# Layer 0 of a two-layer transformer: attention scores moved from one masked 104-row contraction to four 32-row tiles, with queries and keys laid out through DRAM

## What is computed

```python
xn = layernorm(x)                       # no gain, no bias
q = xn @ Wq.T; k = xn @ Wk.T; v = xn @ Wv.T
qh = q.reshape(b, s, 4, 8, 8)           # 4 query heads for each of 8 key heads, head size 8
kh = k.reshape(b, s, 8, 8); vh = v.reshape(b, s, 8, 8)
probs = softmax(einsum('bsqhd,bthd->bqhst', qh, kh) / sqrt(8))
a_dot = einsum('bqhst,bthd->bsqhd', probs, vh)
sigma = elu(q); a_mem = (sigma @ memory) / (sigma @ memory_norm)
x = x + a_dot * (1 - w) + a_mem * w + ffn(xn)   # ffn: 4-bit weights, gelu(gate) * up, hidden 2048
```

## Time and profile before

| | |
|---|---|
| median of 3 runs | 842.98 us (842.37 to 846.78) |
| profiled execution | 845.34 us, span 843.4 us |
| layer 0's units in the trace | unit 0 begins at 28.3 us, unit 63 at 589.2 us |
| TensorE busy | 741.0 us, 88% of the span |
| VectorE, ScalarE, GpSimd busy | 632.9, 468.3, 424.2 us |

### The profile page before, as it was taken

How to read it: one execution, slowest core, us unless ns; L and a number is a source line. 1 busy time by engine, 2 the same in 40 slices (tenths; PEclk the granted TensorE clock), 3 DMA queues, 4 the chain that set the end, 5 groups by cost and what they waited for, 6 DMA issues and landing times. The chain is left out here.

```text
span 843.4 us, 15160 instructions
## 1 busy us (share of the span) xinstructions
PE 741.0 (88%) x5602; PEld 637.2 (76%) x5602; DVE 632.9 (75%) x1099; ACT 468.3 (56%) x746; POOL 424.2 (50%) x369
## 2 busy tenths in 40 slices
PE   3368799999999999999999999999788898889773
PEld 2256678888888887888888888888666687777562
DVE  6989877787777676677768768665264898989865
ACT  4246645655655665564665565657675555565411
POOL 2344354354356566657535434436546373764821
PEclk9579999999999999999999999999979999999985
DMA  5111121111011010110100000021100000000000
GB/s 157 28 39 39 39 77 47 35 50 46 3 33 38 23 40 24 49 40 26 27 10 14 22 2 21 21 78 39 40 14 0 1 1 26 1 26 1 1 26 25
DMA packets 22108, 25.89 MB, mean 31 GB/s; under 512 B 4498, under 2 KB 17170, under 8 KB 22036
## 3 DMA queue, kind: packets, MB, share of 16 engines
q1 hardware_dynamic: 22036, 24.93, 10.4%
HBM read 14.83 MB, written 3.28 MB: 21 GB/s over the span
## 5 line engine op out<-in xcount | busy, mean ns | idle before, releaser
L652 DVE TENSOR_REDUCE neg_max<-s_pair 128x4 f32<-128x1024 f32 x127 | 154.9, 1220 | 75.5 <-PE s_pair L866 75.3
L474 ACT ACTIVATE probs<-t_pair 128x1024 f32<-128x1024 f32 x128 | 131.3, 1025 | 136.4 <-PE t_pair L891 136.2
L371 POOL TENSOR_TENSOR hid<-g,hid 128x512 f32<-128x512 f32 x64 | 82.1, 1283 | 177.8 <-DVE g L763 144.7
L365 POOL TENSOR_TENSOR hid_lo<-hid,hid_hi 128x512 fp32r<-128x512 f32 x64 | 85.5, 1336 | 82.8 <-ACT hid_hi L497 82.7
L866 PE MATMUL s_pair<-K,Q 96*128 96x256 f32 x508 | 85.0, 291 | 15.6 <-DVE neg_max L652 9.3
L866 PEld LDWEIGHTS s_pair<-K,Q 96*128 96x128 f32 x508 | 75.8, 195 | 24.2 <-issue 8.1
L891 PE MATMUL t_pair<-Q,K 104*128 104x512 f32 x256 | 86.2, 418 | 0.3 <-DMA Q<-max_parts 0.3
L933 PE MATMUL down<-hi,hid_hi 128*128 128x256 f32 x256 | 83.9, 328 | 0.8 <-POOL hid_lo L365 0.8
L906 PE MATMUL misc<-probs,V 128*32 128x256 f32 x1024 | 69.4, 389 | 3.3 <-DVE kc L608 2.6
L933 PE MATMUL down<-lo,hid_hi 128*128 128x256 f32 x256 | 71.5, 279 | 0.0
L933 PE MATMUL down<-hi,hid_lo 128*128 128x256 f32 x256 | 71.3, 278 | 0.0
(11 more groups left out here) (258 smaller groups left out, 1964.8 us busy)
## 6 DMA issues: line engine op xcount, KB each, us to landing
stage<-in_ternary SPq DMA_DIRECT2D x18, 256.0 KB, 2.8
Q<-q_hi SPq DMA_DIRECT2D x64, 64.0 KB, 2.0
stage<-in_scales SPq DMA_DIRECT2D x8, 384.0 KB, 3.4
X<-in_x SPq DMA_DIRECT2D x8, 256.0 KB, 4.2
Q<-q_lo SPq DMA_DIRECT2D x32, 64.0 KB, 2.0
Q<-max_parts SPq DMA_DIRECT2D x128, 4.0 KB
out<-X SPq DMA_DIRECT2D x8, 256.0 KB, 2.2
signs<-w_stage SPq DMA_DIRECT2D x9, 128.0 KB, 1.8
```

Of the source, the lines that this page charges most:

```text
L365: pool.tensor_tensor(hid_lo[:, m % 2, :, :].rearrange("p a n -> p (a n)"), hid[:, m % 2, :], hid_hi[:, m % 2, :, :].rearrange("p a n -> p ...
L371: pool.tensor_tensor(hid[:, m % 2, :], g[:, m % 2, :], hid[:, m % 2, :], ALU.mult).then_inc(S["hid_done"], 1)
L474: act.activation(probs[:, u % 2, th, :], t_pair[:], ACT.Exp, scale=SCALE).then_inc(S["probs_done"], 1)
L652: dve.tensor_reduce(neg_max[:, u % 2, 4 * jp:4 * jp + 4], score_banks(u, jp)[:].rearrange("p (s n) -> p s n", n=SEQ), AX_X, ALU.max, negat ...
```

## The change

The scores use row tiles. `Q` and `K` now hold, for each of the 8 key heads, four groups of 32 partitions, one for each query head: 24 rows (three parts x 8) and two for maxima. A score matmul contracts 24 rows of one group, a transposed one 26. So `scores` still has 4 matmuls of 256 columns for each jp, and `scores_turned` now goes by jp and has 4 of 256 columns in place of 2 of 512. To fill this layout, SyncE stores the query parts (6 DMAs) and the keys (1 DMA) of a batch to DRAM and loads each quad with 8 DMAs; GpSimd's masking is gone. Maxima are placed by 4 DMAs in place of 2, and no longer wait for the previous unit. In TensorE's order turn_max(u + 1) comes after the whole gate product, and scores(u + 2, 1) comes last, next to scores_turned(u + 1, 0). VectorE does normalised(u - 1) ahead of maximum(u + 2, 1). The exponential writes the same elements in another order. The weight columns are permuted on the host to match.

The diff, cut:

```diff
@@ schedule @@
-    for kind in ("stats", "norm", "turn", "q", "qlow", "kv", "qload0", "mask0", "qload1", "mask1"):
+    for kind in ("stats", "norm", "turn", "q", "qlow", "kv", "qstore", "kstore", "load0", "load1"):
         put(FIRST, kind, 0)
...
-        for n, kind in ((0, "stats"), (1, "norm"), (2 + late, "turn"), (3 + late, "q"), (4 + late, "qlow"), (4 + late, "qload0"), (4 + late, "kv"),
-                        (5, "mask0"), (5, "recip0"), (6, "recip1"), (8, "qload1"), (8, "mask1")):
+        for n, kind in ((0, "stats"), (1, "norm"), (2 + late, "turn"), (3 + late, "q"), (4 + late, "qlow"), (4 + late, "qstore"), (4 + late, "kv"), (4 + late, "kstore"),
+                        (5 + late, "load0"), (5, "recip0"), (6, "recip1"), (8, "load1")):
@@ layer0, buffers @@
-        Q = sb("Q", [P, 2, QPK, SEQ], F32R)
-        K = sb("K", [P, 2, QUAD, SEQ], F32R)
+        Q = sb("Q", [P, HEADS, SEQ], F32R)
+        K = sb("K", [P, HEADS, SEQ], F32R)
@@ SyncE @@
-            def place_queries(b, quad):
...
-                for r, part in ((0, q_hi), (2, q_hi), (1, q_lo)):
...
-                        sp.dma_start(dst.bitcast(F32), part[src, :, :].bitcast(F32)).then_inc(q_placed[quad], 16)
+            def store_queries(b):
+                sp.wait_ge(S["q_parts"], 3 * b + 1)
...
+                for part, x in ((0, q_hi), (2, q_hi), (1, q_lo)):
+                    if part == 1:
+                        sp.wait_ge(S["q_lo_done"], b + 1)
+                    for jj in range(2):
+                        dst = dram["q_parts"][b % 2, jj::2, DKV * part:DKV * part + DKV, :].rearrange("c e n -> e c n")
+                        sp.dma_start(dst.bitcast(F32), x[DKV * jj:DKV * jj + DKV, :, :].bitcast(F32)).then_inc(S["q_stored"], 16)
+            def store_keys(b):
+                sp.wait_ge(S["kc_lo_done"], b + 1)
...
+                sp.dma_start(dram["k_parts"][b % 2].bitcast(F32), kc[0:KROWS, :, :].bitcast(F32)).then_inc(S["k_stored"], 16)
+            def place_heads(b, quad):
+                if b > 0:
+                    sp.wait_ge(S["st_done"], 2 * (HEADS * (b - 1) + QUAD * quad + QUAD))
+                heads = slice(QUAD * quad, QUAD * quad + QUAD)
+                sp.wait_ge(S["q_stored"], 96 * (b + 1))
+                for r in range(QPK):
+                    src = dram["q_parts"][b % 2, r].rearrange("(e h) n -> e h n", h=HEADS)[:, heads, :]
+                    sp.dma_start(Q[32 * r:32 * r + HROWS, heads, :].bitcast(F32), src.bitcast(F32)).then_inc(qk_placed[quad], 16)
...
+                sp.wait_ge(S["k_stored"], 16 * (b + 1))
+                for r in range(QPK):
+                    src = dram["k_parts"][b % 2].rearrange("(e h) q n -> e q h n", h=QUAD)[:, quad]
+                    sp.dma_start(K[32 * r:32 * r + HROWS, heads, :].bitcast(F32), src.bitcast(F32)).then_inc(qk_placed[quad], 16)
             def place_max(u):
-                if u > 0:
-                    sp.wait_ge(S["st_done"], 2 * u)
...
-                for part in range(2):
-                    sp.dma_start(Q[row + part:row + part + 1, h // QUAD, :, :].rearrange("a q (s n) -> a (q s) n", n=P).bitcast(F32),
-                                 max_parts[:, part, :].bitcast(F32)).then_inc(S["placed"], 16)
+                if u >= HEADS:
+                    sp.wait_ge(S["st_done"], 2 * (u - HEADS) + 2)
+                for s in range(2):
+                    for part in range(2):
+                        sp.dma_start(Q[HROWS + part:P:32, h, P * s:P * s + P].bitcast(F32),
+                                     max_parts[QPK * s:QPK * s + QPK, part, :].bitcast(F32)).then_inc(S["placed"], 16)
@@ GpSimd @@
-                elif kind in ("mask0", "mask1"):
...
-                    pool.tensor_tensor(K[0:KROWS, quad, :, :], src, mask, ALU.mult).then_inc(k_masked[quad], 1)
@@ ScalarE @@
+            act.wait_ge(S["zeroed"], 5)
+            act.activation(K[:].rearrange("p h n -> p (h n)"), ones[:, 0:1].to_broadcast([P, HEADS * SEQ]), ACT.Copy).then_inc(S["rows_set"], 1)
@@ VectorE, the unit loop @@
+                if attends(u - 1):
+                    normalised(u - 1)
                 if attends(u + 2):
                     maximum(u + 2, 1)
                 if u == FIRST + 1:
                     weights_low(0)
-                if attends(u - 1):
-                    normalised(u - 1)
@@ TensorE, scores @@
                 if jp == 0 and hq == 0:
-                    pe.wait_ge(q_placed[quad], 96 * (b + 1))
-                    pe.wait_ge(k_masked[quad], b + 1)
+                    pe.wait_ge(qk_placed[quad], 128 * (b + 1))
...
-                for j in range(2):
-                    for s in range(2):
-                        mm = pe.matmul(score_banks(u, jp)[:, 512 * j + SEQ * s:512 * j + SEQ * s + SEQ], Q[0:KROWS, quad, 2 * jp + j, P * s:P * s + P],
-                                       K[0:KROWS, quad, hq, :], start=True, stop=True)
+                for s in range(2):
+                    for j in range(2):
+                        rows = slice(32 * (2 * jp + j), 32 * (2 * jp + j) + HROWS)
+                        mm = pe.matmul(score_banks(u, jp)[:, 512 * j + SEQ * s:512 * j + SEQ * s + SEQ], Q[rows, h, P * s:P * s + P], K[rows, h, :], start=True, stop=True)
@@ TensorE, scores_turned @@
-                for jp in range(2):
-                    mm = pe.matmul(t_pair[:, 512 * jp:512 * jp + 512].rearrange("p (j n) -> p j n", j=2), K[rows, quad, hq, P * th:P * th + P],
-                                   Q[rows, quad, 2 * jp:2 * jp + 2, :], start=True, stop=True)
+                for th in range(2):
+                    for j in range(2):
+                        rows = slice(32 * (2 * jp + j), 32 * (2 * jp + j) + HROWS + MROWS)
+                        mm = pe.matmul(t_pair[:, 512 * j + SEQ * th:512 * j + SEQ * th + SEQ], K[rows, h, P * th:P * th + P], Q[rows, h, :], start=True, stop=True)
@@ TensorE, the unit loop @@
-                    hidden_product(m, 0, gate, S["gate_done"], u + 1 if attends(u + 1) else None)
-                elif attends(u + 1):
+                    hidden_product(m, 0, gate, S["gate_done"])
+                if attends(u + 1):
                     turn_max(u + 1)
                 before = steps(u)
...
                 if 0 <= m - BEHIND < M:
                     down_product(m - BEHIND, 0)
-                if attends(u + 2):
-                    scores(u + 2, 1)
                 if attends(u - 1):
                     turn_out(u - 1)
                 if 0 <= m - BEHIND < M:
                     down_product(m - BEHIND, 1)
+                if attends(u + 2):
+                    scores(u + 2, 1)
```

More of the change, by code:

```diff
@@ L60 @@
 KROWS = 3 * QUAD * DH
-MROWS = 2 * QUAD
+HROWS, MROWS = 3 * DH, 2
 CW = WORDS // 2
@@ L178, in layer0 @@
         S = {n: ctx.enter_context(nc.semaphore(f"a_{n}")) for n in names}
-        q_placed, k_masked = ([S[f"{n}{i}"] for i in range(2)] for n in ("q_placed", "k_masked"))
+        qk_placed = [S[f"qk_placed{i}"] for i in range(2)]
         stage_sem = [S[f"stage{i}"] for i in range(2)]
@@ L267, in _ @@
                 for kind, n in at.get(u, []):
-                    if kind in ("qload0", "qload1"):
-                        place_queries(n, int(kind[-1]))
+                    if kind == "qstore":
+                        store_queries(n)
+                    elif kind == "kstore":
+                        store_keys(n)
+                    elif kind in ("load0", "load1"):
+                        place_heads(n, int(kind[-1]))
                 a = u + 3
@@ L399, in _ @@
                 for kind, n in at.get(u, []):
-                    if kind == "mask1" and u == FIRST:
+                    step(kind, n)
+                    if kind == "qlow" and u == FIRST:
                         weights_low(0)
-                    step(kind, n)
                     if kind == "recip0" and u == -1:
@@ L429, in step @@
                     if b > 0:
-                        for quad in range(2):
-                            act.wait_ge(k_masked[quad], b)
+                        act.wait_ge(S["k_stored"], 16 * b)
                         act.wait_ge(S["v_turned"], b)
@@ L446, in query_parts @@
                 if b > 0:
-                    for quad in range(2):
-                        act.wait_ge(q_placed[quad], 96 * b)
+                    act.wait_ge(S["q_stored"], 96 * b)
                     act.wait_ge(S["sigma_done"], 2 * b)
@@ L657, in split_max @@
                 if u > 0:
-                    dve.wait_ge(S["placed"], 32 * u)
+                    dve.wait_ge(S["placed"], 64 * u)
                 dve.tensor_copy(max_parts[:, 0, :], misc[0:8, 2 * P:3 * P]).then_inc(S["dve_link"], 1)
@@ L878, in turn_max, with scores_turned @@
                 pe.transpose(misc[0:8, 2 * P:3 * P], neg_max[:, u % 2, :], ident[:]).then_inc(S["max_turned"], 1)
[L880 removed]
+            def scores_turned(u, jp):
                 b, h = divmod(u, HEADS)
                 quad, hq = divmod(h, QUAD)
[L883 to L892 removed]
+                if jp == 0:
```

(30 more changed lines are left out.)

59 lines of the change are left out of this document (17 added, 42 removed).

## The result

871.39 us in the median of four runs (866.85 to 872.38) against 844.88 (842.37 to 847.71, four runs here, three in the table ahead). The ratio is 1.0305, 95% interval 1.0259 to 1.0352: slower by 3%. The profiled executions are 866.85 (span 865.1) and 845.34 (span 843.4), 21.7 apart in span. Forecast was +38, measured +26.5 between the medians.

The account below looks back on a forecast made before the run. Past the first units TensorE's own work was taken to bound the kernel. Terms -26 + 28 + 2 + 17 + 8 + 7 + 5 - 3 = +38 gave 881 us for the median, range 850 to 922.

Parts of the forecast that it names:

- late turn: Steps behind turn_max after the whole gate product start later: +0.71 us in 40 units past the first six, +28 us.
- row stretches: Two TensorE stretches of 8 score matmuls per unit, 0.73 us each, replace 1.90 us: -26 us over units 6 to 63.
- third wave: Each stretch of 8 score matmuls was counted as three waves of 0.118 us, 0.35, plus 0.38 around them.
- loads of batches 2 to 7: TensorE waits 2.9 us ahead of each such batch's first scores for queries and keys through DRAM: +17 us.
- Turn_out: Turn_out loses scores(u+2, 1) as its cover, and ScalarE's copy is late where VectorE is: +2 us in all.
- Unit 6: Batch 1's load0 stands behind place_max(7) in the very iteration that needs it: +8 us.
- separate term for the clock: Seven stops of 3 to 8 us bring three falls of the granted clock: +5 us (0 to 12).
- Start: First scores wait for stores and loads through DRAM until 26.2 us, VectorE's decoding behind them: +7 us, all counting.
- GpSimd: Without masks GpSimd has the sigmas earlier, so one or two waits ahead of mem go: -3 us.
- waits smaller, stretches at 0.6: Rival: loads issue at 0.43 us, no clock falls, stretches at 0.6: 851 us; smaller waits or cheaper stretches, chance 0.12.

Follow-up runs that it names:

- experiment 1: The kernel before, with only turn_max moved behind the whole gate product: 881.57 us, ratio 1.0447 to the kernel before.
- experiment 2: The changed kernel's layout, tiles and DMAs in the order of the kernel before: 861.93 us, ratio 1.0217 to the kernel before.
- Experiment 8: The changed kernel with only VectorE's two reciprocals of a batch moved behind its second gelu operation: 870.18 us, ratio 1.0295 to the kernel before.
- 5: The changed kernel with TensorE's steps moved behind scores_turned(u, 1) and scores(u+2, 0): 855.09 us, ratio 1.0134 to the kernel before.
- 6: The changed kernel without stores and loads of queries and keys for batches 1 to 7, which use batch 0's: 852.58 us, ratio 1.011 to the kernel before.
- 7: The changed kernel with batch 1's load0 in iteration 5, not 6: 864.34 us, ratio 1.0237 to the kernel before.
- 9: experiment 2 with SyncE's transfers spread (high query parts and load0's queries earlier, batch 1's keys in iteration 5): 841.22 us, ratio 0.9962 to the kernel before.
- 10: The changed kernel with steps behind the second stretch, reciprocals behind VectorE's second gelu operation, and SyncE's transfers spread: 824.48 us, ratio 0.9771 to the kernel before.

## Why the prediction was right in its direction and too high

- **The late turn was right:** 0.71 forecast, 0.68 measured ahead of each of the 40 steps, and experiment 1 gives the 28 us by itself. What I did not price is VectorE's own lateness: in experiment 1 it costs another 10 us; in the changed kernel it is turn_out's wait.
- **The row stretches were mis-sized:** two at 0.73 forecast, from three waves. There are two waves, and 0.63 less two of 0.12 leaves 0.39 around them: the 0.38 for entrance and exit was right, the third wave was not. Unit 58 fell by 0.61, not 0.44; 0.62 over 58 units is -36 and not -26. I had let `t_pair`'s first matmuls start beside `s_pair`'s second ones, which holds if matmuls start in program order. The Trainium skill ("TensorE: Matmul & The Clock Gate", Part 3) says both that row tiles start about 4 ns apart and that matmuls start and end strictly in program order. The first agrees with the trace (0.01 us). The second doesn't: `t_pair`'s first matmuls start at 574.39, and `s_pair`'s second ones, which stand ahead of them in the program, at 574.61. Its "TensorEngine Tiling (Array Packing)", Key Properties, where a change of mode drains the engine, does agree: the eight matmuls stream two waves of 0.12 and the stretch takes 0.63, and four alone take 0.62 (experiment 2).
- **The gain did not reach all units.** Units 59 to 61 stayed at 7.67 us. In 59 turn_out comes 0.5 us late. In 60 and 61 the trace names 0.2 us, but the starts show more: VectorE does 2 us of work for layer 1's weights ahead of the split of the maxima, which ends 2.45 us after turn_max and not 0.9, and `weighted` needs the bank that the split reads. In unit 60 it starts 0.28 us late, turn_out behind it 0.16, and the transposed half of the next stretch 0.12 behind its other half. The split and `weighted` there:

```profile
593.26 0.28 DVE L666 TENSOR_TENSOR max_parts<-misc,max_parts 8x128 fp32r<-8x128 f32 x1
593.64 1.07 PE L908 MATMUL misc<-probs,V 128*32 128x256 f32 x16 [0.21 <-issue]
```

- **The loads of batches 2 to 7 were mis-sized,** 2.9 us each forecast and 0.34 to 1.37 measured, 5.7 in all and not 17. The landing time was right (12.5 us into the fifth unit, counted from its transposed scores; 334.43 - 321.98 = 12.45 in unit 29). The step that failed is the time at which TensorE asks for them: I took a fifth unit of 7.24 us and it was 8.54, as turn_out waited 1.24 there. Experiment 8 takes that wait away and gives 2.89. Two waits in a row don't add when the second is for something that lands at a fixed time: the first hides part of it.
- **Turn_out** was given 2 us in all and costs 1.24 in each of four fifth units and 1.83 in unit 13. It stands ahead of the loads' wait and takes most of it over. The two terms together came near, though each was wrong, as the landing time fixes what the fifth and sixth unit take together: 19 forecast; measured 5.4 + 7.4 by the table, plus the 12 x 0.62 that these units saved, less the 1.8 that unit 46 lost to its clock, 18.4.
- **Unit 6:** +8 forecast, +8.9 measured. The wait is 10.81 us, and the granted clock is at half its speed for 13.7 us from 112.9 on; the window's 0.66 shows it. That fall was in my separate term for the clock (+5), which else brought one short one (unit 46) and one less (unit 31).
- **Start:** +7 forecast. The first scores came at 26.59 where I had 26.2, but VectorE has other decoding to do meanwhile, and the gate of unit 1 is 4.1 late. I had said that all of it would count, and 4.1 of it did.
- **GpSimd:** -3 forecast, -4.9 measured: both waits ahead of mem, 1.5 us each in units 31 and 39, are gone, and with the first of them the clock fall of unit 31, 1.9 us.

In one sum, +38 to +21.7 in span: stretches -10, start and units 1 to 5 -2, the separate clock term -3 (1.8 in unit 46 for 5), GpSimd -2, the late turn -1, and +1 for unit 6, -1.5 for v, whose transposes in 32 rows now run beside a stretch (8.28 to 8.06 in its unit); units 59 to 61 took back 2. Between medians the miss is smaller, as the four runs of the changed kernel lie up to 5.5 above the profiled one. The rival "waits smaller, stretches at 0.6" (851) had the stretches right and the size of the loads' term, but not for its reason (0.43 us an issue; the keys' loads take 0.82); it lacked turn_out, which took the loads' place.

Shown: what each part does by itself (1, 2, 5 to 9), and that they go together (10). Only argued: that v gains by running beside a stretch, and, from starts in the trace alone, why units 60 and 61 gained nothing. Open: how much of the runs' spread (866.85 to 872.38) is the clock.

## What to carry to other kernels

When a small result must go over another engine, write down its cover (which matmuls run meanwhile) before moving it, and after each move ask for the next user of the same bank: the 0.96 us here moved from gate to the steps (0.68), and then to `weighted` (0.71). Where an edit removes a wait and the time stays, look for a transfer that lands at a fixed time behind it; repair both or neither pays (8 alone nothing that shows, 7 alone 7 us, all covers together 47). Small matmuls in row tiles pay when several share one stretch, not when each has its own: every stretch has its entrance and exit, some 0.39 us here, and four matmuls cost as much as eight.

## What the runs showed of the hardware that I had not expected

- Row groups take their matmuls from the program independently within a stretch of eight: both orders gave two waves (574.38 and 574.61; 577.08 and 577.31). The 128-column weight loads of the two pairs overlap too: two each, begun at 574.38 and 574.39, 0.18 us long.
- SyncE's issue cost differs from transfer to transfer. In unit 6, four placing DMAs (4 partitions each), four loads of queries and four of keys (both 96 KB into 24 partitions, from differently laid out rows in DRAM):

```profile
112.26 2.23 SPq L268 DMA_DIRECT2D Q<-max_parts  x4
114.61 1.61 SPq L252 DMA_DIRECT2D Q<-q_parts  x4
116.26 3.27 SPq L258 DMA_DIRECT2D K<-k_parts  x4
```

  So 0.56, 0.40 and 0.82 us each; units 21 and 29 show the same within 0.01. What in the layout makes the difference no run shows. I had taken 0.68 for all; the eight loads, 5.4 so, took 4.9.
- A stop of 1 to 3 us is sometimes followed by a fall of the granted clock (unit 46 of the changed kernel after 1.37 us, units 22, 30, 38, 46 and 54 of experiment 8 after 1.6 to 2.9) and sometimes not (units 29 and 30 of the changed kernel: 1.24 idle in each, clock 1.00 in 322.43 to 330.96 and through unit 30). No run here tells the two apart.
